# A per-sample weight mix moved out of the tile loop: one product, a round trip through DRAM, and a reordered x on GpSimd

## What is computed

```python
att = softmax(h @ W2 + b2)                       # 128 samples x 8
agg_w = einsum('bk,koi->boi', att, weight)       # a 32x32 mixing matrix per sample
y = einsum('boi,bih->boh', agg_w, x) + agg_b
x1 = x + y @ W_up.T + lora_of_top1(y)            # layer 0
c = grouped_conv1d(x1, 9 taps) + ctx             # layer 1
out = x1 + c @ W_base.T + b_base + lora_of_top2(c)
```

## Time and profile before

| | us |
|---|---|
| median of 3 runs | 380.35 (377.62 to 380.48) |
| the profiled execution | 379.92 |
| its span, first to last instruction | 378.1 |
| mean granted TensorE clock | 0.986 of full speed |

### The profile page before, as it was taken

One profiled execution on the slowest core, in us unless ns is written; L12 is line 12 of the kernel. 1 busy time (PEld: TensorE's weight loads), 2 busy tenths in 40 slices (PEclk: granted clock), 3 DMA queues, 4 the chain that ended last, 5 costly groups with the idle time before them and its releaser, 6 DMA issues.

```text
span 378.1 us, 8986 instructions
## 1 busy us (share of the span) xinstructions
PE 356.5 (94%) x2589; PEld 343.6 (91%) x2589; DVE 284.5 (75%) x966; ACT 135.5 (36%) x409; POOL 179.4 (47%) x223
## 2 busy tenths in 40 slices
PE   2877999999999999999999999999999999999975
PEld 1666999999999999999999999999999999999964
DVE  1675768787887887777788788777877878877653
ACT  2634243333333434433333343443333333343321
POOL 5364455544445455554444545555444454444430
PEclk9998699999999999999999999999999999999999
DMA  7622245343323323333332333333333233234221
GB/s 163 187 85 30 93 123 149 86 85 76 62 59 78 76 72 81 84 84 84 84 59 59 74 77 73 77 84 84 84 84 78 42 74 78 72 77 86 56 58 56
DMA packets 49983, 30.92 MB, mean 82 GB/s; under 512 B 39684, under 2 KB 40116, under 8 KB 49968
## 3 DMA queue, kind: packets, MB, share of 16 engines
q1 hardware_dynamic: 35744, 26.60, 28.2%
q10 hardware_dynamic: 13984, 3.73, 6.6%
q0 software_dynamic: 240, 0.41, 0.4%
HBM read 13.79 MB, written 8.40 MB: 59 GB/s over the span
## 4 chain that ended last, share of the span: by engine, by line
PE 86%; DVE 2%; POOL 1%; ACT 1%; DMA 1%; issue 1%; ACTq 1%; DVEq 0%; POOLq 0%
PE ps_base L1004 21%; PE ps_up L854 17%; PE ps_base L1009 10%; PE ps_up L859 8%; PE ps_mix L914 7%; PE ps_conv L876 6%; PE ps_mix L876 6%; PE ps_base L987 6%; PE ps_up L901 2%; PE ps_turn L893 1%; DMA xq<-x1s 1%; PE ps_turn L885 1%; ACTq L277 1%; POOL base_p L388 1%; PE ps_base L814 1%
## 5 line engine op out<-in xcount | busy, mean ns | idle before, releaser
L430 POOL TENSOR_TENSOR y_lo<-y,y_hi 128x512 fp32r<-128x512 f32 x31 | 40.1, 1295 | 141.0 <-ACT y_hi L478 141.0
L1004 PE MATMUL ps_base<-base_hi,c_hi 128*128 128x392 f32 (+1 forms) x256 | 78.6, 323 | 2.5 <-ACT c_hi L526 1.3
L1004 PE MATMUL ps_base<-base_lo,c_hi 128*128 128x392 f32 (+1 forms) x256 | 75.2, 311 | 0.0
L854 PE MATMUL ps_up<-up_hi,y_hi 128*128 128x292 f32 (+1 forms) x256 | 72.2, 304 | 1.2 <-ACT y_hi L478 1.2
L854 PE MATMUL ps_up<-up_lo,y_hi 128*128 128x292 f32 (+1 forms) x256 | 69.5, 293 | 0.0
L581 DVE TENSOR_TENSOR mix_w<-gsum,quad 128x64 f32<-128x64 f32 x64 | 39.2, 616 | 33.2 <-PE ps_base L1009 32.1
L415 POOL TENSOR_TENSOR xq_lo<-xq,xq_hi 128x260 fp32r<-128x260 f32 x64 | 46.6, 745 | 34.5 <-ACT xq_hi L507 24.8
L422 POOL TENSOR_TENSOR x1b<-x1s,bbase_s 128x256 f32<-128x256 f32 x64 | 57.0, 923 | 0.0
L1004 PEld LDWEIGHTS ps_base<-base_hi,c_hi 128*128 128x128 f32 x256 | 48.2, 188 | 8.2 <-issue 4.8
L854 PEld LDWEIGHTS ps_up<-up_hi,y_hi 128*128 128x128 f32 x256 | 49.2, 192 | 1.4 <-ACT y_hi L478 1.3
L478 ACT ACTIVATE y_hi<-y 128x512 fp32r<-128x512 f32 x32 | 20.2, 632 | 82.2 <-DVE y L591 78.9
(11 more groups left out here) (164 smaller groups left out, 639.5 us busy)
## 6 DMA issues: line engine op xcount, KB each, us to landing
xt<-in_x SPq DMA_DIRECT2D x32, 256.0 KB, 2.8
out_x<-ot SPq DMA_DIRECT2D x32, 256.0 KB, 2.8
xq<-x1s SPq DMA_DIRECT2D x160, 32.5 KB, 2.2
xq<-x1s ACTq DMA_DIRECT2D x96, 32.5 KB, 2.2
rows<-agg_rows SPq DMA_DIRECT2D x2, 597.0 KB, 3.9
wbase_raw<-in_L_ffn_W_base SPq DMA_DIRECT2D x2, 512.0 KB, 4.3
rows<-agg_rows SPq DMA_DIRECT2D x1, 598.0 KB, 4.0
wup_raw<-in_L_ffn_W_up ACTq DMA_DIRECT2D x2, 256.0 KB, 4.6
```

The lines of the kernel that those rows point to most:

```text
L430: pool.tensor_tensor(y_lo[:], y32[:], y_hi[:], ALU.subtract).then_inc(ylo_done, 1)
L854: pe.matmul(into, y_hi[:, k], w[:, k, cols], start=(k == 0 and w is up_hi), stop=False, skip_group_check=True)
L1004: pe.matmul(ps_base[:, j, 0:width], c_hi[:, q], w[:, q, j, 0:width], start=(q == 0 and w is base_hi), stop=False, skip_group_check=True)
```

## The change

**Weights of tiles 5 to 31.** The weight tensor is loaded a second time as wk_s (8 x 1024, one issue more on SP ahead of the base weights). At the end of step 0 PE makes the mixing matrices of all 128 samples with two products attT x wk_s of 512 columns each, in the banks ps_conv and ps_turn. ACT and DVE copy them out with input and output channel swapped (mix_b), and PE waits for both copies before its first convolution. SP writes mix_b to DRAM behind step 1 and reads it back in steps 2 and 3 with four transfers, one per sample of a tile, onto the diagonal blocks of mix_all (128 x 32 tiles x 128), which POOL has set to zero at the start. PE waits for all four at the end of step 3. From tile 5 on `mix` reads its weights out of mix_all. Tiles 0 to 4 are made as before.

**DVE.** Where a part of `mix_sums` or `mix_blocks` stood, a memset of one column (beat) stands from then on. `x1_sum` reads xtp, a copy of x in x1's order.

**POOL.** `order_x(i+1)` makes that copy, where `make_prod` stood. Its wait for the load of x of tile i+1 stands at the head of the step, ahead of the two xq_lo.

**ACT** makes xq_hi's first half, then the exponential of the second gate, then the second half.

**PE** transposes zm behind the second product of `up_half(i, 0)` in place of the fourth. The loop covers steps 4 to 29.

```diff
-        FIRST, LAST = 4, NT - 4
+        FIRST, LAST = 4, NT - 2
 ...
+            sp.dma_start(wk_s[:], wmix.rearrange("k o i a -> k (o i a)")).then_inc(in_wk, 16)
             load_base(0)
 ...
+                if isinstance(i, int) and i == 1:
+                    sp.wait_ge(mixb_ready, 2)
+                    sp.dma_start(mix_dram, mix_b[:].rearrange("b i o -> b (i o)")).then_inc(mixb_out, 16)
+                if isinstance(i, int) and i in (2, 3):
+                    if i == 2:
+                        sp.wait_ge(mixb_out, 16)
+                        sp.wait_ge(mix_zero, 1)
+                    for s in range((i - 2) * SPT // 2, (i - 1) * SPT // 2):
+                        rows_s = slice(s * C, (s + 1) * C)
+                        sp.dma_start(mix_all[rows_s, :, rows_s],
+                                     mix_dram.rearrange("(t s) (i o) -> s i t o", s=SPT, o=C)[s]).then_inc(mix_in, 16)
 ...
+            pool.memset(mix_all[:], 0.0).then_inc(mix_zero, 1)
 ...
+            def order_x(t, par):
+
+                pool.tensor_copy(xtp[:, par].rearrange("p (j r m) -> p j r m", j=2, r=NQ), columns_of(xt[:, par]))\
+                    .then_inc(xtp_done, 1)
 ...
+            pool.wait_ge(x_in[0], 16)
+            order_x(0, 0)
             pool.wait_ge(in_b1, 16)
 ...
             def body(i, par):
                 if once(i - 1):
 
+                    if once(i + 1):
+                        pool.wait_ge(x_in[1 - par], (i + par) * 8 + 16)
                     for gp in range(GP):
                         pool.wait_ge(xqhi_done, 2 * i - 1 + gp)
 ...
-                if once(i + 3):
+                if isinstance(i, int) and i + 3 < SOON:
                     make_prod(i + 3)
+                if once(i + 1):
+                    if not once(i - 1):
+                        pool.wait_ge(x_in[1 - par], 16)
+                    order_x(i + 1, 1 - par)
 ...
+                if once(i - 1):
+                    x_high(i, 0)
                 if once(i - 2):
 
                     act.wait_ge(m81_ready, i - 1)
                     act.activation(e2[:], m81[:, 0:1], ACT.Exp, bias=m81[:, 1:2], scale=-1.0).then_inc(e2_ready, 1)
                 if once(i - 1):
-
-                    for gp in range(GP):
-                        act.wait_ge(xq_in[gp], i * XQ)
-                        after(act, conv_done, 2 * i - 3 + gp)
-                        act.activation(xq_hi[:, gp], xq[:, gp], ACT.Copy).then_inc(xqhi_done, 1)
+                    x_high(i, 1)
 ...
+                    act.wait_ge(mixb_done, 1)
+                    act.activation(mix_columns(0), ps_conv[:, 0].rearrange("b (o i) -> b o i", i=C), ACT.Copy)\
+                        .then_inc(mixb_ready, 1)
 ...
+                dve.wait_ge(xtp_done, t + 1)
                 for j in range(2):
                     dve.wait_ge(lb_done, 2 * t + j + 1)
                     dve.tensor_tensor(shifted(j), ps_up[:, j, 0:HALF].rearrange("p (r m) -> p r m", r=NQ),
-                                      columns_of(xt[:, par])[:, j], ALU.add).then_inc(x1_done, 1)
+                                      xtp[:, par, j * HALF:(j + 1) * HALF].rearrange("p (r m) -> p r m", r=NQ),
+                                      ALU.add).then_inc(x1_done, 1)
 ...
-                    if once(i + 1):
+                    if soon(i + 1):
                         mix_blocks(i + 1, 0)
+                    else:
+                        dve.memset(beat[:], 0.0)
                     dve.max(m81[:], logits).then_inc(m81_ready, 1)
 ...
+                    dve.wait_ge(mixb_done, 2)
+                    dve.tensor_copy(mix_columns(1), ps_turn[:, 0].rearrange("b (o i) -> b o i", i=C))\
+                        .then_inc(mixb_ready, 1)
                     dve.wait_ge(consts_ready, 1)
                     dve.wait_ge(fill_lo, NF)
                     dve.tensor_copy(slots, iota8[:]).then_inc(slots_ready, 1)
 ...
-                    if k == KC // 2 and turn is not None:
+                    if k == 1 and turn is not None:
                         turn(t)
 ...
-                pe.wait_ge(mixw_done, (t + 1) * 2)
+                if isinstance(t, int) and t < SOON:
+                    pe.wait_ge(mixw_done, (t + 1) * 2)
+                    weights = mix_w[:].rearrange("p b o -> p (b o)")
+                else:
+                    weights = mix_all[:, bass.ds(t, 1), :].rearrange("p t o -> p (t o)")
 ...
+                    pe.wait_ge(in_wk, 16)
+                    pe.wait_ge(fill_lo, NF2)
+                    for half, to in enumerate((ps_conv, ps_turn)):
+                        pe.matmul(to[:, 0], attT[:], wk_s[:, half * H:(half + 1) * H], start=True, stop=True)\
+                            .then_inc(mixb_done, 1)
 ...
+                if isinstance(i, int) and i == FIRST - 1:
+                    pe.wait_ge(mix_in, 16 * SPT)
```

More of the change, by code:

```diff
@@ L40 @@
 EARLY = 4 * P
+SOON = 5
 REST = 3
@@ L50, in adaln_ffn @@
     rows_dram = nc.dram_tensor("agg_rows", [B * C], F32, kind="Internal").ap()
+    mix_dram = nc.dram_tensor("agg_mix", [B, C * C], F32, kind="Internal").ap()
     with ExitStack() as ctx:
@@ L118, in adaln_ffn @@
         mix_w = sb("mix_w", [P, SPT, C])
+        wk_s, mix_b = sb("wk_s", [KATT, C * C]), sb("mix_b", [B, C, C])
+        mix_all = sb("mix_all", [P, NT, P])
+        xtp = sb("xtp", [P, 2, H])
+        beat = sb("beat", [P, 1])
         y32, y_hi, y_lo = sb("y32", [P, KC, P]), sb("y_hi", [P, KC, P], F32R), sb("y_lo", [P, KC, P], F32R)
@@ L167, in adaln_ffn @@
         upgate_done, basegate_done = sem("upgate_done"), sem("basegate_done")
+        in_wk, mixb_done, mixb_ready, mixb_out, mix_in = (sem("in_wk"), sem("mixb_done"), sem("mixb_ready"),
+                                                          sem("mixb_out"), sem("mix_in"))
+        mix_zero, xtp_done = sem("mix_zero"), sem("xtp_done")
         lb_done, x1_done, x1b_done = sem("lb_done"), sem("x1_done"), sem("x1b_done")
@@ L230, in once, with soon @@
             return not isinstance(tile, int) or 0 <= tile < NT
+        def soon(tile):
+            return isinstance(tile, int) and tile < SOON
         def after(eng, sem, count):
@@ L273, in adaln_ffn, with mix_columns @@
         ps_of = (ps_conv, ps_mix)
+        def mix_columns(half):
+            return mix_b[:, :, half * C // 2:(half + 1) * C // 2].rearrange("b i o -> b o i")
         def move_x(eng, gp, b):
@@ L460, in high_part, with x_high @@
                     act.activation(fills[n][4], fill_bank(n), ACT.Copy).then_inc(fill_hi, 1)
+            def x_high(i, gp):
+                act.wait_ge(xq_in[gp], i * XQ)
+                after(act, conv_done, 2 * i - 3 + gp)
+                act.activation(xq_hi[:, gp], xq[:, gp], ACT.Copy).then_inc(xqhi_done, 1)
             def z_high(t):
@@ L743, in body @@
                         ALU.mult, ALU.mult).then_inc(hw_done, 1)
-                elif once(i + 1):
+                elif soon(i + 1):
                     mix_blocks(i + 1, 0)
@@ L752, in body @@
                     dve.wait_ge(gate0_step, i * G0 + 1)
-                    if once(i + 2):
+                    if soon(i + 2):
                         mix_sums(i + 2, 0)
+                    else:
+                        dve.memset(beat[:], 0.0)
                     dve.max(m80[:], gl0[:]).then_inc(gate0_step, 1)
                     dve.wait_ge(gate0_step, i * G0 + 2)
-                    if once(i + 2):
+                    if soon(i + 2):
                         mix_sums(i + 2, 1)
+                    else:
+                        dve.memset(beat[:], 0.0)
                     dve.max_index(ix0[:], m80[:], gl0[:]).then_inc(gate0_step, 1)
@@ L913, in mix @@
                 for k in range(KC):
-                    mm = pe.matmul(ps_mix[:, 0, k * P:(k + 1) * P], xt[:, par, k * P:(k + 1) * P],
-                                   mix_w[:].rearrange("p b o -> p (b o)"), start=True, stop=True)
+                    mm = pe.matmul(ps_mix[:, 0, k * P:(k + 1) * P], xt[:, par, k * P:(k + 1) * P], weights,
+                                   start=True, stop=True)
                 mm.then_inc(mix_done, 1)
@@ L964, in body @@
                     pe.wait_ge(fill_lo, NF)
+                    pe.wait_ge(mixb_ready, 2)
                     pe.wait_ge(slots_ready, 1)
```

## The result

The changed kernel takes 407.51 us (median of 4 runs, 406.51 to 409.44), the kernel before 380.17 (4 runs): a ratio of 1.0741, 95% interval 1.068 to 1.0803. The profiled execution took 406.51 us, its span is 404.7, its mean granted TensorE clock 0.992. So 7.4% is lost, though PE has no more work to do than before. Each ratio in this document is estimated from the undisturbed runs alone, leaving out the few that were some per cent longer at a lower granted clock, so it can differ a little from the ratio of the medians given.

The account below looks back on a forecast made before the run. PE bounded the kernel before (10.48 us a step); the wait for x would bound the changed one (11.3). 46.2 + 316.4 + 17.8 + 10.2 + 18.3 gives span 408.9, with 1.8 around it 410.7: forecast 411, range 395 to 424.

Parts of the forecast that it names:

- E30: A moment, not a run: the end of x1_sum of tile 30, forecast at 380.4 us, 349.4 in the kernel before.
- E31: A moment, not a run: the end of x1_sum of tile 31, forecast 10.2 us after E30 and 18.3 before the end.
- The circle through the load of x: In the loop, xq_lo waits for x, whose load is issued behind SP's moves: 11.3 us a step, bounds 10.9 and 11.7.
- rival 3: In the loop, the load of x lands at 3.2 us: 11.7 us a step, 422 us; chance 0.18 together with Rival 4.
- x1_sum and the gap: On DVE, the copy shortens x1_sum by 0.43 us; PE's 8.2 us gap at the base product goes nearly whole.
- Rival 4: On DVE, x1_sum stays at 636 ns: chain 11.7 us a step, 422 us; chance 0.18 together with rival 3.
- Rival 1: In the loop, x is no wait: 379.5 us, or 371.5 if mix_in is no wait either; chance 0.06 each.
- The copy on POOL: In each step POOL copies x in 1.28 us, beside PE, adding nothing to the step.
- The stop for mix_in: At the loop's entry PE stands 5.6 us for mix_all's reads, +4.5 us, plus 2 us for a lower clock.
- Rival 2: At the loop's entry, mix_in doesn't bind, its reads landing within 5 us of E3: 404 us; chance 0.15.
- The start: Before the loop, two products take PE 1.8 us, first convolution at about 40.5, x1_sum of tile 1 ends at 46.2.
- The exponential: On ACT, placed after the first half of xq_hi, it costs nothing because that half of xq is in well before.

Follow-up runs that it names:

- late use: Changed kernel with POOL's wait moved behind both xq_lo and mix_all first used for tile 7 in place of 5: 373.55 us, ratio 0.9832.

## Why the prediction was right, point by point

Forecast 411, measured 407.5, by the mechanism that was named. E is, as in the prediction, the end of x1_sum; SP's moves start 0.03 us behind it, and by their starts E1 is 43.89, E3 65.79, E4 82.18, E30 376.97 and E31 387.33.

**The circle through the load of x.** Right, and shown from four sides: take the wait away (ratio 0.9961), take away what stands ahead of the load (0.9966), add the wait alone to the kernel before (1.1043), put it half way (1.0136). Its links in the turn above, forecast against measured: load issued at E + 3.67 against 222.11 - 218.39 = 3.72; POOL at E + 6.7 against 225.00 - 218.39 = 6.61; PE's load 0.83 behind POOL against 214.61 - 213.82 = 0.79; from there to E 3.82 against 218.39 - 214.61 = 3.78. x landed a median of 2.8 us after its issue, as before, so rival 3 (3.2) is out. The loop's 26 steps from E4 (82.18) to E30 (376.97) took 11.34 us each, forecast 11.3. PEld's wait was forecast as 28 times about 1.1 us and came as 28 times, 29.9 us. x1b on POOL, ahead of x1_sum, added nothing, as reckoned.

**x1_sum and the gap.** 420 ns against 420; the step that PE would set is 10.22, forecast 10.2. In the changed kernel this gain sits inside the circle, which is why the kernel before with the wait alone is slower than the change. Rival 4, an x1_sum that stays at 636 ns, falls with it. Rival 1 was right in its working, though its condition never arose: with the wait harmless it gave 379.5, and the two kernels that make it so took 378.2 and 378.8.

**The copy on POOL.** 1196 ns for a forecast 1.28 us, hidden.

**The stop for mix_in.** The mechanism was right, the size somewhat high. Queue, loop entry and PE's records:

```profile
69.59 1.04 SPq L366 DMA_DIRECT2D mix_all<-agg_mix  x2
...
74.72 0.58 PE L917 MATMUL ps_up<-up_hi,y_hi 128*128 128x292 f32 x1 [4.56 <-DMA mix_all<-agg_mix]
75.10 0.45 PE L917 MATMUL ps_up<-up_lo,y_hi 128*128 128x292 f32 x1
75.34 0.45 PE L917 MATMUL ps_up<-up_hi,y_hi 128*128 128x292 f32 x1
```

PE stood 4.56 us, forecast 5.6. SP issued the second pair at 69.59, 3.8 us after E3 (65.79), and they were in at E3 + 8.9, forecast 9.6; the four landed in 3.8 to 5.0 us, forecast 5.0. Behind the stop the products start 0.24 us apart in place of 0.135 and the granted clock is 0.50 from 74.72 to 77.80, the 1.2 GHz level; by these starts that costs some 1.4 us, forecast 2. From E3 to E4 that made 16.39 us, forecast 17.8. The difference is within what the kernels with this stop show among themselves: in their five profiles PE stood 4.2 to 5.8 us, and E3 to E4 took 16.3 to 19.1. Rival 2, no stop, is out. Its price by the pairs that differ in it is 1.3% (0.9961 to 0.9832) and 1.1% (1.0167 to 1.0059), 4 to 5 us.

**The start.** PE's timeline, then three stretches (columns as above), and the first of these three in the kernel before and in the kernel before with the wait alone:

```profile
34.19 1.09 PE L1068 MATMUL ps_conv<-wk_s,attT 8*128 8x512 f32 x2 [0.22 <-DVE base_lo L615]
...
38.97 0.77 PE L939 MATMUL ps_conv<-xq_hi,conv_hi 128*128 128x256 f32 x2 [0.39 <-DVE ps_base L860]
```

```profile
27.70:32.70 5.00, 4.06 (x34) 3.81 (x35) 2.87 (x6) 2.33 (x5) 5.00 (x8) 1.00 0.01 3
37.20:40.50 3.30, 2.91 (x13) 2.59 (x13) 3.21 (x11) 0.74 (x3) 2.29 (x4) 0.50 0.60 232
37.40:44.15 6.75, 6.36 (x42) 6.04 (x42) 6.07 (x21) 2.40 (x10) 4.93 (x6) 0.77 0.26 102
```

```profile
27.70:32.70 5.00, 4.29 (x24) 4.04 (x25) 2.00 (x4) 2.44 (x5) 3.58 (x6) 0.71 0.01 3
```

```profile
27.70:32.70 5.00, 3.48 (x29) 3.23 (x30) 2.70 (x6) 2.33 (x5) 4.17 (x7) 1.00 0.01 3
```

The two products took PE 1.95 us (34.19 to 36.14), forecast 1.8, and the copies 1.16 and 1.07 us, forecast 1.11. But the first convolution came at 38.97, not at 40.5, and E1 at 43.89, not at 46.2. That is the largest single miss, and it is luck of the profiled execution, not a gain of the change. The granted clock was 1.00 from 27.70 to 32.70, before either of the two products, where the kernel before had 0.71. Four of the kept profiles have 1.00 there, and E1 at 43.9 to 45.0; two of them are kernels without these products (the wait alone and the copy alone, both in the kernel before). Nine others have 0.50 to 0.71, and E1 at 45.3 to 47.3, around the forecast. What decides between the two is not shown. Nor does 0.77 in place of 0.50 from 37.40 to 44.15 show that the products kept the clock up: the kernel before with the wait alone has 0.80 there without them.

**The sum.** Against the forecast span of 408.9: E1 -2.3, the steps to E3 (21.9 for 22.6) -0.7, E3 to E4 -1.4, the loop +1.0, tile 31 (10.36 for 10.2) +0.2, the end (17.4 for 18.3) -0.9. Together -4.1, which is the measured 404.7 within 0.1. More than half of it is the lucky start. The stretch at the end was copied from the kernel before; why it came out shorter is told below.

**What was put at nothing.** The weights and the freed DVE and POOL time: nothing, as forecast. The transpose: nothing shown. The exponential was put at nothing because "the first half of xq is in well before it". That is the step that failed, though little hung on it in the sum. It holds in the loop. In step 32 it doesn't, and what it costs depends on when the first half of xq is in. In the profile of the changed kernel ACT makes xq_hi's first half at E31 + 3.0, and PE's transpose of hw starts at E31 + 4.7. The four kernels that differ from it only in the wait's place, the load's place or the copy show the same two times:

```profile
390.36 0.42 ACT L509 ACTIVATE xq_hi<-xq 128x260 fp32r<-128x260 f32 x1 [3.27 <-DMA xq<-x1s]
...
391.99 0.33 PE L948 MATMUL ps_turn<-ident,hw 128*128 128x128 f32 x1 [0.41 <-DVE hw L796]
```

With ACT's old order the transpose starts at E31 + 4.3 to 4.4, so the new order cost the changed kernel some 0.3 us there. Its stretch from E31 to the end is even shorter, 17.4 for 18.3 us, since xq was in earlier: ACT made the second half at E31 + 4.7, 5.6 before. In the kernels with late use and the new order, and in the kernel before with the new order, the first half came only at E31 + 4.3 to 5.1, and the transpose started at 5.9 to 6.7. That is where the 1.5 to 2.3 us come from. The wait for x is not what makes the difference, since the kernels without its harm have the 0.3 us too. Why xq lands early in one set of kernels and late in the other was not tried.

**Put together**, as shares of the kernel before that add up through the kernels run: the wait's place +7.8% (1.0741 to 0.9961), the copy -2.1% (1.0167 to 0.9961), the stop +1.1% (1.0167 to 1.0059), and the weights' route with its new orders +0.6% (1.0059 to 1), of which a part may be the exponential and the rest is open. Sum 7.4%. Each ratio has an interval of 0.2 to 0.6% either way, so the last two are known only roughly.

## What to carry to other kernels

Before a wait is put at the head of a queue, follow it to the issue that ends it and count what stands ahead of that issue on its own queue: a load "of the step before" may be issued later than it looks, and if the queued work behind the wait leads back to the same issue, the wait sets the loop's step. Put a wait right ahead of its first user; here, two instructions further down was worth 29 us. Work taken off engines that don't set the step was worth nothing, and an order that is free in the loop has to be looked at again in the last written-out steps, where the operands come at other distances.

## What the runs showed that was not expected

A read of 128 KB in 1024 pieces of 128 bytes from DRAM landed in 3.8 to 5.0 us with a median of 4.6, about as long as the 256 KB in as many pieces of 256 bytes from POOL's queue: the count of pieces, not the bytes, seems to set it, though no run here varied the two apart.

The moves of the last tile brought the first half of xq in at E31 + 3.0 in five of the profiles and at 4.3 to 5.1 in the four others with ACT's new order, and a term of 1 to 2 us hung on it. SP's five issues took 3.1 us in the five, 3.8 to 3.9 in three of the four and 3.1 in the last, so the issues alone don't explain it, and its cause stays open.

SP's issues were in the prediction, but their size is worth a second look. Five moves take it 3.45 us, 0.69 each, before the issue of the next transfer even starts; that is more than the 2.8 us in which a load of 256 KB lands. On this queue the order of issues was worth as much as the size of a transfer.
